# Graph kernel on one core: moments moved to VectorE, large loads to other queues, node blocks 17 columns apart, a seventh ring place

## The reference, cut to what matters

```python
h = maximum(layernorm(x), 0)
x_ij = concatenate([h[src], h[dst]], axis=1)
x = x + segment_sum(relu(x_ij @ L0_W.T + b), src)       # layer 0
h = maximum(layernorm(x), 0)
out = segment_sum((h @ L1_W.T)[src] * edge_weight[:, None], dst)
x = x + where(out >= 0, out, alpha * out)               # layer 1
```

## Time and profile before

| | us |
|---|---|
| median of 3 runs | 1019.98 |
| lowest, highest of the runs | 1013.48, 1021.19 |
| the profiled execution | 1017.97 |
| its span | 1016.2 |
| first stage in it, up to L655 | 271.9 |

### The profile page before, as it was taken

How to read it: one execution, slowest core, us unless ns; L and a number is a source line. 1 busy time by engine, 2 the same in 40 slices (tenths; PEclk the granted TensorE clock), 3 DMA queues, 4 the chain that set the end, 5 groups by cost and what they waited for, 6 DMA issues and landing times.

```text
span 1016.2 us, 20178 instructions
## 1 busy us (share of the span) xinstructions
PE 972.9 (96%) x4719; PEld 781.0 (77%) x4720; DVE 872.2 (86%) x1747; ACT 775.0 (76%) x1650; POOL 643.0 (63%) x934
## 2 busy tenths in 40 slices
PE   5799999999799999999999999999999999999998
PEld 5477778787678887788878778878888788778776
DVE  6989988897769999999999999999999888873444
ACT  4887878778788888888888888888888776755210
POOL 2478877767477777777777777777777755530000
PEclk9689999899989999999999999999999999999999
DMA  8000000000021111111111111111111100010011
GB/s 220 4 3 4 2 4 2 4 2 3 19 62 42 44 42 41 40 42 43 41 43 42 40 40 41 43 42 41 44 41 42 31 30 30 24 42 1 21 41 40
DMA packets 35923, 35.16 MB, mean 35 GB/s; under 512 B 7778, under 2 KB 32095, under 8 KB 35876
## 3 DMA queue, kind: packets, MB, share of 16 engines
q1 hardware_dynamic: 31176, 33.95, 10.7%
q0 software_dynamic: 4416, 0.30, 1.7%
q10 hardware_dynamic: 284, 0.33, 0.1%
HBM read 30.92 MB, written 3.29 MB: 34 GB/s over the span
## 4 chain that ended last, share of the span: by engine, by line
PE 68%; DVE 2%; ACT 1%; issue 1%; POOL 0%; POOLq 0%
PE node_ps L1166 8%; PE edge_ps L1205 8%; PE edge_ps L1211 8%; PE edge_ps L1210 8%; PE edge_ps L1206 8%; PE node_ps L1167 8%; PE m_ps L1177 4%; PE psum L1309 3%; PE psum L1311 3%; PE psum L1310 3%; PE m_ps L1291 1%; PE edge_ps L1269 1%; PE edge_ps L1270 1%; PE edge_ps L1261 1%; PE edge_ps L1266 1%; PE edge_ps L1265 1%
## 5 line engine op out<-in xcount | busy, mean ns | idle before, releaser
L1398 ACT ACTIVATE msg_hi<-edge_ps 128x512 fp32r<-128x512 f32 x332 | 197.6, 595 | 60.8 <-PE edge_ps L1211 60.7
L1122 POOL TENSOR_TENSOR M<-M,pair_w 125x125 f32 x332 | 160.7, 484 | 126.9 <-DVE pair_w L1545 97.2
L1559 DVE SCALAR_TENSOR_TENSOR msg_lo<-edge_ps,msg_hi 128x512 fp32r<-128x512 f32 x332 | 223.6, 683 | 17.3 <-ACT msg_hi L1398 13.0
L417 POOL DMA_INDIRECT edge_table<-fields,row_no x136 | 170.4, 1253 | 58.2 <-issue 47.4
L844 ACT ACTIVATE lane_piece<-hot_lane,fields 125x128 fp32r<-125x128 bf16 x498 | 153.8, 392 | 12.1 <-DVE hot_lane L504 11.8
L705 PE MATMUL psum<-hot_tile,lane_piece 125*128 125x384 f32 x582 | 145.8, 373 | 9.2 <-ACT lane_piece L844 6.3
L1106 POOL TENSOR_TENSOR hot_w<-hot_d,weight_l 128x252 fp32r<-128x252 bf16 x166 | 140.0, 843 | 0.0
L1166 PE MATMUL node_ps<-msg_hi,hot_s 128*125 128x512 f32 x332 | 135.1, 407 | 0.0
L1205 PE MATMUL edge_ps<-b_hi,turned_d 125*128 x332 | 132.7, 400 | 0.7 <-ACT turned_d L1382 0.7
L1211 PE MATMUL edge_ps<-a_lo,turned_s 125*128 x332 | 131.9, 397 | 0.0
L1210 PE MATMUL edge_ps<-a_hi,turned_s 125*128 x332 | 131.4, 396 | 0.2 <-ACT turned_s L1382 0.2
(11 more groups left out here) (258 smaller groups left out, 2044.8 us busy)
## 6 DMA issues: line engine op xcount, KB each, us to landing
spread<-edge_rows SPq DMA_DIRECT2D x190, 125.0 KB
out_dram<-result SPq DMA_DIRECT2D x10, 224.0 KB
edge_table<-fields,row_no POOLq DMA_INDIRECT x136
w_in<-in_L_gnn_W_dram SPq DMA_DIRECT2D x1, 2048.0 KB, 12.7
S<-in_x_dram SPq DMA_DIRECT2D x1, 1792.0 KB
w_in<-in_L_gnn_W_dram SPq DMA_DIRECT2D x1, 1024.0 KB, 5.1
S<-in_x_dram SPq DMA_DIRECT2D x1, 448.0 KB
edge_table<-zeros SPq DMA_DIRECT2D x1, 384.0 KB, 14.9
```

Of the source, the lines that this page charges most:

```text
L417: pool.indirect_dma_start(table_dram[:, :], bass.IndirectOffsetOnAxis(ap=row_no[:, c:c + 1], axis=0), fields[:, c, 0:TABLE_FIELDS], None). ...
L1122: pool.tensor_tensor(part, part, pair_w[h][:, j, 0, 0:BN], ALU.add).then_inc(m_added, 1)
L1398: act.activation(msg_hi[j][:], edge_ps[j][:], ACT.Relu).then_inc(hi_ready, 1)
L1559: dve.scalar_tensor_tensor(out=msg_lo[j][:], in0=edge_ps[j][:], scalar=0.0, in1=msg_hi[j][:].bitcast(F32), op0=ALU.max, op1=ALU.subtract). ...
```

## The change

- Moments: ACT's passes are gone. DVE's moment(b, stage) does bn_stats, bn_aggr, reciprocal and the product for shift, each as a step of its own, and ACT's deviation(b) does the square root between the second and the third. Block 0's steps stand behind hot blocks 6 and 7 and behind picks 8 and 10 of chunk 0, those of block b from 1 on at columns 17 b - 15, 17 b - 14, 17 b - 6 and 17 b - 5, with the root on ACT at 17 b - 13. A square root on a dummy value now stands first on ACT.
- Loads: the weights (w_in, 2 MB) and blocks 2 to 9 of x (2 MB) are started by ACT, behind dst and edge_weight and ahead of all its other work; the clearing of the table by POOL, behind the memset of zeros. SP keeps src, blocks 0 and 1 of x and the small ones.
- Weights: the eight pieces of pairs 2 and 3 stand behind prefix products 1, 2, 4, 5, 7, 8, 10 and 11 of chunk 0.
- Blocks: STEP is 17. normal 1, turn 3, high copy 7, low_of_h 11, product 12; high copies 22 and 26, low 24 and 28, low copies 28 and 32.
- RING is 7. To make room, h1 lies in the second half of planes, and some small tensors are gone.

```diff
-RING = 6
+RING = 7
+WEIGHTS_AMONG = [1, 2, 4, 5, 7, 8, 10, 11]
-STEP = 16
-NORMAL_AT, TURN_AT, ROUND_AT, REST_AT, PRODUCT_AT = 2, 5, 8, 12, 13
-HI_AT, LOW_AT, LO_AT = (19, 23), (23, 26), (27, 29)
+STEP = 17
+MOMENTS_AT, STD_AT = (2, 3, 11, 12), 4
+NORMAL_AT, TURN_AT, ROUND_AT, REST_AT, PRODUCT_AT = 1, 3, 7, 11, 12
+HI_AT, LOW_AT, LO_AT = (22, 26), (24, 28), (28, 32)
...
+            planes_room = sb1("planes_room", [EROWS, PICK * CHUNK + D], F32)
+            planes = planes_room[:, 0:2 * PICK * CHUNK].rearrange("p (b c) -> p b c", c=CHUNK)
+            h1 = planes_room[:, PICK * CHUNK:PICK * CHUNK + D]
...
 # SP
-                    for part, blocks in enumerate(X_PARTS):
-                        for rows in SPLIT:
-                            sp.dma_start(S[rows, blocks], ...).then_inc(x_in[part], 16)
-                        if part == 0:
-                            sp.dma_start(w_in[:], ...).then_inc(w_loaded, 16)
+                    for rows in SPLIT:
+                        sp.dma_start(S[rows, X_PARTS[0]], ...).then_inc(x_in[0], 16)
...
-                    sp.wait_ge(cleared, 1)
-                    sp.dma_start(table_dram[...], zeros...).then_inc(cleared_dram, 16)
 # POOL, behind memset(zeros)
+                    pool.wait_ge(cleared, 1)
+                    pool.dma_start(table_dram[...], zeros...).then_inc(cleared_dram, 16)
 # DVE
+                    def moment(b, stage):
+                        if stage == 0:
+                            dve.wait_ge(x_in[0 if b < X_PARTS[0].stop else 1], 32)
+                            dve.bn_stats(stats[:, b, :], S[0:BN, b, :]).then_inc(moments, 1)
+                            return
+                        dve.wait_ge(moments, 4 * b + stage)
+                        if stage == 1:
+                            dve.bn_aggr(mv[:, b, :], stats[:, b, :]).then_inc(moments, 1)
+                        if stage == 2:
+                            dve.wait_ge(std_ready, b + 1)
+                            dve.reciprocal(rstd[0:BN, b:b + 1], std[:, b:b + 1]).then_inc(moments, 1)
+                        if stage == 3:
+                            dve.scalar_tensor_tensor(out=shift[0:BN, b:b + 1], ...).then_inc(moments, 1)
...
                     for s in range(6, NBLK):
                         hot_of_block(0, s)
+                        if s < 8:
+                            moment(0, s - 6)
...
                         pick(0, g)
+                        if g in (8, 10):
+                            moment(0, g // 2 - 2)
...
-                            if k == 0 and i == 1:
-                                ... rstd and shift of all blocks
+                            b, stage = divmod(q + STEP, STEP)
+                            if 0 < b < NBLK and stage in MOMENTS_AT:
+                                moment(b, MOMENTS_AT.index(stage))
 # PE
+                    def weights_part(n):
+                        pair, part = divmod(n, 4)
+                        (turn_w, turn_w, low_w, low_w)[part](2 * (pair + 2) + part % 2)
...
                         prefix(0, g)
-                    weights(2)
-                    weights(3)
+                        if g in WEIGHTS_AMONG:
+                            weights_part(WEIGHTS_AMONG.index(g))
 # ACT
+                    act.dma_start(w_in[:], ...).then_inc(w_loaded, 16)
+                    for rows in SPLIT:
+                        act.dma_start(S[rows, X_PARTS[1]], ...).then_inc(x_in[1], 16)
+                    act.wait_ge(dconst, 1)
+                    act.activation(std[:, 0:1], eps_t[0:BN, :], ACT.Sqrt)
...
-                    act.wait_ge(x_in[0], 32)
-                    moments(range(2))
                     copy_counts(0)
...
                     copy_counts(1)
-                    act.wait_ge(x_in[1], 32)
-                    moments(range(2, NBLK))
-                    ... one Sqrt for all blocks
+                    deviation(0)
                     turned_weights(2)
                     turned_weights(3)
...
+                                if stage + STEP == STD_AT and b > 0:
+                                    deviation(b)
                                 if stage == NORMAL_AT:
-                                    if b == 0:
-                                        act.wait_ge(rstd_ready, 2)
+                                    act.wait_ge(moments, 4 * b + 4)
                                     normal(b)
```

More of the change, by code:

```diff
@@ L297, in build @@
             act_own = sem("act_own")
+            moments = sem("moments")
             std_ready = sem("std_ready")
-            rstd_ready = sem("rstd_ready")
             w_ps = sem("w_ps")
@@ L511, in column @@
                                                      op0=ALU.is_equal, op1=ALU.mult).then_inc(dve_pieces, 1)
+                    def moment(b, stage):
[10 more added lines that the diff above has]
+                        if stage == 3:
+                            dve.scalar_tensor_tensor(out=shift[0:BN, b:b + 1], in0=mv[:, b, 0:1], scalar=-1.0,
+                                                     in1=rstd[0:BN, b:b + 1], op0=ALU.mult, op1=ALU.mult).then_inc(moments, 1)
                     def low_of_h(b):
@@ L555, in _ @@
                     dve.tensor_copy(iota_h[:], iota[:, 0:P])
-                    dve.memset(planes[:], 0.0).then_inc(planes_clear, 1)
+                    dve.memset(planes, 0.0).then_inc(planes_clear, 1)
                     dve.wait_ge(totals, 1)
@@ L848, in normal @@
                     def normal(b):
-                        act.activation(h1[:], S[0:BN, b, :], ACT.Relu, bias=shift[0:BN, b:b + 1],
+                        act.activation(h1, S[0:BN, b, :], ACT.Relu, bias=shift[0:BN, b:b + 1],
                                        scale=rstd[0:BN, b:b + 1]).then_inc(h_ready, 1)
@@ L866, in _, with deviation @@
                     ins.then_inc(grouped, 1)
-                    steps = [2]
-                    def step(ins):
-                        steps[0] += 1
-                        ins.then_inc(act_own, 1)
-                        act.wait_ge(act_own, steps[0])
-                    def moments(blocks):
-                        for b in blocks:
-                            step(act.activation(h1[:], S[0:BN, b, :], ACT.Identity, accum_out=sums[:, 0, b:b + 1]))
-                        these = slice(blocks[0], blocks[-1] + 1)
-                        step(act.mul(neg_mean[0:BN, these], sums[:, 0, these], -1.0 / D))
-                        for b in blocks:
-                            step(act.activation(h1[:], S[0:BN, b, :], ACT.Square, bias=neg_mean[0:BN, b:b + 1],
-                                                accum_out=sums[:, 1, b:b + 1]))
+                    def deviation(b):
+                        act.wait_ge(moments, 4 * b + 2)
+                        act.activation(std[:, b:b + 1], mv[:, b, 1:2], ACT.Sqrt, bias=eps_t[0:BN, :]).then_inc(std_ready, 1)
                     def turned_weights(pair):
@@ L902, in _ @@
                     copy_counts(1)
-                    act.wait_ge(x_in[1], 32)
-                    moments(range(2, NBLK))
-                    act.wait_ge(dconst, 1)
-                    act.activation(sums[:, 2, :], sums[:, 1, :], ACT.Sqrt, bias=eps_t[0:BN, :],
-                                   scale=1.0 / D).then_inc(std_ready, 1)
+                    deviation(0)
                     turned_weights(2)
```

17 lines of the change are left out of this document (5 added, 12 removed).

## The result

The median is 1023.7 us over 8 runs (1021.0 to 1029.4), beside 1016.85 us of the kernel before over 8 runs in the same comparison. The ratio is 1.0075, with a 95% interval of 1.0045 to 1.0106. The prediction had 1018.0 and "within 1%". The time lies in the range given, but the forecast was no change, and the kernel is 7 us slower. The profiled execution took 1023.22 us, its span 1021.5. The table is decoded at 279.61 us for 271.94. The rest is 741.9 us for 744.3, so in this pair all of the loss is in the first stage.

A forecast was written before the change was run, and what follows sets the result against it. Bound: the coupled DVE, ACT, PE column chain, with POOL's transfers close behind, before L655 at 271.9 us. Start delays and shorter chunks summed to 271.0, 0.9 less: 1017.1 us profiled, 1018.0 median; range 1009 to 1026.

The forecast's parts named there:

- ACT held by the starts: Start of kernel: load starts hold ACT from about 3 to between 8 and 9 us, making prefix 0 3.1 us late.
- Weights among the prefixes: Chunk 0: picks done 14.2 us after prefix 0 instead of 8.5, so its slots come 5.7 us later again.
- rival A: Start: ACT is not held, everything 4.5 us earlier; median 1013.5, at best 1008 to 1010; chance 0.28.
- Slots of chunk 1 at 93.1: End of chunk 0's columns: these slots end at 93.1 us against 86.6 before, 6.5 us late.
- The moments: DVE among the columns: 1.1 us a block, 9.9 for nine blocks; 2.2 in chunk 0, 2.4 in each of three more.
- Copies later, STEP 17, ring 7: Column phase: ACT's 9.0 us of waits for b_hi and its like should go, with part of PE's wait for pieces.
- Full chunks of 45.3 us: Chunks after chunk 0, before the last: DVE's floor of 43.7 us plus 1.6 for coupling, against 47.1 on average before.
- The last window: Last chunk's columns, after slots 4 end at 229.0: 42 us with fewer waits, against 44.2 before.
- the forecast 271.0: End of the first stage: L655 starts at 271.0 us by the columns, 0.9 less than 271.9 before.
- C: Column phase: late copies change nothing, ACT waits at low copies instead; 47 to 48 us a chunk, 1023.5; chance 0.15.
- B: Full chunks: DVE becomes the bound and each moment lengthens the chunk; 13.8 us more, 1031.8; chance 0.07.

The follow-up runs named there:

- the two kernels placed by slots: Node blocks at uneven columns (0, 15, 32 up to 158) instead of every 16: in the kernel before 1.0064; in the changed kernel, with later count copies, 1.0075.

## Why the prediction was wrong, step by step

- **ACT held by the starts: right, and dearer.** Forecast 5 to 6 us and by_group ending at 14.8; it was 6.99, and 15.6. Prefix 0 came at 30.94, 1.2 late and not 3.1. The section of the Trainium skill that the prediction weighed (DMA: Bandwidth & Descriptors, Issuing engines are not separate DMA queues) calls the time to start a transfer usually small beside the transfer itself. The start of w_in agrees, 0.40 us with 14.4 to its landing; the two starts behind it held ACT 6.99 us, and no row has their landing. But the hold cost nothing at the end: with the loads on SP again the ratio was the same, 1.0076.
- **Weights among the prefixes: the price was taken from a row at half clock.** Forecast 3.62 us for two turned tiles and picks that last 14.2 us. A tile takes 1.05 us at PEclk 1.00, the picks were done 9.9 us after prefix 0 (30.94 to 40.8), and POOL's first transfer came at 46.21, not at 52.5. PEclk beside the row would have told it. This part came out nearer to rival A, though ACT was held.
- **Slots of chunk 1 at 93.1: they were at 84.1, 9.0 us early.** The reference too was off: eight profiles of kernels with the old start have their first column at 47.9 to 51.1 us, so the true gain of the start is about 1 to 4 us where the profile of before suggests 5.6, and by the end of chunk 0 nothing is left of it. The moments were sized rightly, 1.13 us a block; but 2.2 in chunk 0 and 2.4 in each of three more make 9.4, not 9.9.
- **Copies later, STEP 17, ring 7: this is the step that failed.** It has the new plan shorten the full chunks by 1.8 us each, from 47.1 to 45.3, and the last from 44.2 to 42. The plan alone, in the kernel before, costs 5.5 us. The next two points are its two terms.
- **Full chunks of 45.3 us: they took 46.8, 49.3 and 51.3 us,** 11.4 more in sum. The wait for b_hi went, as the step says, but ACT's waits at the counts and at the turned h came, and nothing was won: at full clock the three take 136.0, and 135.9 before. That 136.0 is also three times 45.3 is luck, for the 45.3 was a gain on windows in which the clock was already below full. The term for the clock was missing. The prediction had PEclk 1.00, 0.96 and 0.93 for them in front of it in the earlier trace rows, and neither its sum nor a rival says what more or fewer dry spells of PE would do to it.
- **The last window: "with fewer waits 42".** From the end of slots 4 at 231.4 it took 48.2, 6.2 more than forecast. I counted for it that no moment lies there and did not count which node work does. The window begins where slots 4 end, and these stand at column 144, not at 152. Block 8's products have moved from columns 141 to 148 to columns 148 to 155, so in the window PE has all 24 of them for 15 before, besides block 9's 24. The prediction says "its work is the same before and after" of PE, which holds for the whole stage and not for the chunk in which PE is the longest engine. Together: 9.0 early, 11.4 and 6.2 late is the 8.6 us between L671 at 279.6 and the forecast 271.0.
- **Rivals.** C had the right time, 1023.5, for the wrong reason: the wait for b_hi did go. B had its mechanism in part. The moments do cost, but not by filling DVE. The run without them says 6 us, and the windows of one pair of profiles say that most of it went through the clock. None of the rivals was that the new plan itself is slower, and that plan alone is 5.5 of the 7 us.

The parts don't add up exactly. Plan alone +6 thousandths, moments +6 (or +3 at pitch 16), seventh place -2, and the start -1 to nothing, make 6 to 10 for 7.5; copies and plan may share one loss. With intervals of 2 to 3 thousandths each, the shares are known to that, no better.

That a part of the loss goes by the clock is supported by the runs and not by the profiles alone. Over the 14 to 32 runs of the kernel before in each group, a run with a mean clock 0.001 higher is 0.45 to 0.86 us shorter. The kernel before with pitch 17 alone has a mean of 0.9752 over 8 runs where the kernel before has 0.9791 over 18, which at that group's 0.86 is 3.3 us of the 5.9 between their means. The one without moments has 0.9834 over 11 runs where the one with the loads on SP has 0.9789 over 8, which at that group's 0.71 is 3.2 us of the 5.6 between their means. It is still a correlation; no run set the clock. And it is not the whole: the two kernels placed by slots have more clock than the kernel before beside them (0.981 and 0.984 for 0.979) and are 6 to 8 us slower; their last chunk is 5.4 and 5.7 us longer.

## What to carry to other kernels

Before work is moved inside a list of steps, cut the list where the pace changes hands (here at column 144, where the last picks and slots end) and count each engine's instructions on both sides: here work moved onto the side where its own engine is the longest was paid for, though the total was unchanged. Read the granted clock beside every TensorE row before its duration is used as a price, and give a plan that makes TensorE run dry a term for the half clock behind it. And look at the start of several executions: one profile's 5 us can be that execution's own.

## What the runs showed of the hardware that was not expected

- A phase in which PE is busy 91 to 95% of the time still loses 3 to 13% of its clock in single chunks. The drop comes around waits of only 2 to 3 us (2.42, 2.96 and 1.90 us in the profile after), and once already ahead of the long one: in the windows above PE was busy 1.32 of 2.0 us, then the mean clock was 0.61, and the wait of 2.96 us came behind. The Trainium skill (TensorE: Matmul & The Clock Gate, A second HAM failure mode: psum-queue depth-cycling) tells of a kernel whose short pauses between groups of matmuls take the clock down again and again; these rows agree with it.
- The two starts of x blocks 2 to 9 (2 MB together), behind 2 MB of weights on one queue, held ACT 6.99 us after (5.99 to 7.51 in nine profiles) and SP 5.10 before (4.19 to 6.30 in eleven). A start is not always a fraction of a microsecond.
- The last chunk takes 44.2 to 44.3 us in all six profiles with pitch 16, with either kernel's other parts, while chunks 1 to 3 of the same kernels take 138.3 to 145.0 us. In the last chunk PE is busy for 42.2 to 42.7 us and PEclk is 1.00 in all six; in chunks 1 to 3 PEclk falls to 0.90.
